# Second projection of both MLPs with the weights stationary and 400 tokens moving

## The reference, cut to what matters

```python
# layer 0
out = rmsnorm(attn_out, postnorm_w)
out = jax.nn.gelu(out @ mlp_w1 + mlp_b1) @ mlp_w2 + mlp_b2
return out + residual
# layer 2
h = _layer_norm(x, ln_mlp_scale, ln_mlp_offset)
h = jax.nn.gelu(h @ w_fc1 + b_fc1, approximate=False) @ w_fc2 + b_fc2
return x + h
```

## Time and profile before

| | |
|---|---|
| median of 3 runs | 4184.49 us (4182.9 to 4185.43) |
| the profiled execution | 4186.43 us, of which its span is 4184.7 us |
| mean granted clock of PE | 0.921 of full speed |
| PE, DVE, ACT, POOL busy | 85%, 39%, 28%, 13% of the span |
| first MLP: first matmul to end of last add | 616.2 to 780.5 us |
| second MLP: first matmul to end of last add | 3508.8 to 3672.4 us |

### The profile page before, as it was taken

The page is one execution under the profiler, slowest core; times in us unless marked ns, Lnnn a source line. Parts: engine busy times, 40 slices in busy tenths (PEclk is TensorE's granted clock), DMA queues, the critical chain, the costliest instruction groups (busy, mean ns, idle before and its releaser), DMA issues. The chain is left out here.

```text
span 4184.7 us, 50251 instructions
## 1 busy us (share of the span) xinstructions
PE 3566.8 (85%) x18055; PEld 2780.5 (66%) x18055; DVE 1639.4 (39%) x3090; ACT 1156.1 (28%) x2700; POOL 559.9 (13%) x479
## 2 busy tenths in 40 slices
PE   4999979796665789898998969989899997968886
PEld 3777758553333378787887858878787885846663
DVE  2454442316876232323223242232323324136654
ACT  2343343121002122222222222222222223235551
POOL 0000020023441300000000020000000001044432
PEclk9999989898987889999999979999999998977777
DMA  2111111000000041222222122121212212021101
GB/s 88 50 36 38 39 49 46 29 20 3 0 10 31 12 127 50 80 56 87 57 61 62 42 85 67 50 87 49 87 42 81 57 28 83 1 73 40 40 22 32
DMA packets 142028, 209.06 MB, mean 50 GB/s; under 512 B 18915, under 2 KB 104356, under 8 KB 141932
## 3 DMA queue, kind: packets, MB, share of 16 engines
q0 software_dynamic: 67584, 94.64, 8.7%
q1 hardware_dynamic: 74348, 113.17, 8.6%
HBM read 191.04 MB, written 13.47 MB: 49 GB/s over the span
## 5 line engine op out<-in xcount | busy, mean ns | idle before, releaser
L63 PE MATMUL work<-cT_layer_hi,wk_layer_hi 128*128 128x362 f32 x1024 | 390.3, 381 | 0.0
L1908 ACT ACTIVATE p_layer<-scores,neg_max_layer 100x362 f32<-100x362 f32 x256 | 144.3, 564 | 740.6 <-DVE neg_max_layer L1963 739.3
L64 PE MATMUL work<-cT_layer_lo,wk_layer_hi 128*128 128x362 f32 x1024 | 336.9, 329 | 0.0
L65 PE MATMUL work<-cT_layer_hi,wk_layer_lo 128*128 128x362 f32 x1024 | 336.6, 329 | 0.0
L1944 DVE TENSOR_TENSOR values_layer<-work,value_bias_layer 121x512 f32<-121x512 f32 x192 | 132.4, 690 | 519.4 <-PE work L65 519.4
L63 PE MATMUL work<-wv_layer_hi,cT_layer_hi 128*121 128x512 f32 x768 | 311.9, 406 | 0.0
L64 PE MATMUL work<-wv_layer_lo,cT_layer_hi 128*121 128x512 f32 x768 | 303.3, 395 | 0.0
L65 PE MATMUL work<-wv_layer_hi,cT_layer_lo 128*121 128x512 f32 x768 | 302.5, 394 | 0.0
L1751 POOL DMA_DIRECT2D cT_layer_hi<-ctxT_hi x64 | 47.7, 745 | 1745.6 <-PE work L65 1743.3
L1820 PE MATMUL o<-pT_layer,values_layer 121*128 121x100 f32 x1536 | 215.9, 277 | 56.9 <-ACT pT_layer L1914 56.9
L1820 PEld LDWEIGHTS o<-pT_layer,values_layer 121*128 121x128 f32 x1536 | 205.5, 191 | 87.5 <-ACT pT_layer L1914 70.2
(11 more groups left out here) (358 smaller groups left out, 7430.9 us busy)
## 6 DMA issues: line engine op xcount, KB each, us to landing
cT_layer_hi<-ctxT_hi POOLq DMA_DIRECT2D x64, 722.0 KB, 4.9
cT_layer_lo<-ctxT_lo POOLq DMA_DIRECT2D x64, 722.0 KB, 6.2
l0mlp_staged<-in_L_xattn_mlp_w_dram SPq DMA_DIRECT2D x16, 512.0 KB, 4.2
staged_layer<-in_L_xattn_wq_dram SPq DMA_DIRECT2D x8, 1024.0 KB, 5.2
staged_layer<-in_L_xattn_wk_dram SPq DMA_DIRECT2D x8, 1024.0 KB, 5.2
staged_layer<-in_L_xattn_wv_dram SPq DMA_DIRECT2D x8, 1024.0 KB, 5.2
staged_layer<-in_L_xattn_wo_dram SPq DMA_DIRECT2D x8, 1024.0 KB, 5.4
l2mlp_staged<-in_L_xattn_w_fc_dram SPq DMA_DIRECT2D x16, 512.0 KB, 4.2
```

Of the source, the lines that this page charges most:

```text
L63: pe.matmul(out, cut_a(a.hi), cut_b(b.hi), start=start, stop=False)
L64: pe.matmul(out, cut_a(a.hi), cut_b(b.lo), start=False, stop=False)
L65: return pe.matmul(out, cut_a(a.lo), cut_b(b.hi), start=False, stop=stop)
L1908: act.activation(probs[x % 4][:, 0:KEYS2], ps_scores[x % 2][0:L, 0:KEYS2], ACT.Exp, bias=neg_max[:, x:x + 1], accum_out=sums[:, x:x + 1]). ...
```

## The change

In `use` the two operands of the second projection change places: the weights `down_w` (128 hidden x 128 output features) are stationary, and the 400 tokens of a half move. For each of the 4 tiles of output features (`m`) and 2 tiles of hidden features there are 3 matmuls, so 24 as before. The sums then have output features on the partitions and must be turned back: at the end of a half ACT copies the banks m = 0, 2 and DVE the banks m = 1, 3 from PSUM to the first 400 columns of the four `staged` buffers (`copy_sums`); PE transposes them, 4 transposes for each batch, into a bank in the layout of `k.X` (`turn`); DVE adds that bank to `k.X` (`add`).

PSUM is dealt out anew: 3 banks for the first projection, 4 for the sums, 1 (`ps_token`) for the transposes. The first five batches use `ps_token` one after the other; the last three use the three banks of the first projection, which are then free. `turn` of the first half stands inside the steps 9 and 10, between the products: turn(0) and turn(1) in step 9 before use(8), turn(2) after it, turn(3) in step 10. Those of the second half stand at the end. `make` is called for one tile at a time, and waits for the gelu of tile n - 3. DVE's adds of the first half stand between its splits of `gT` in the steps 9 and 10 (`ADD_AT`).

```diff
--- before.py
+++ after.py
@@ -741,7 +741,9 @@
     CHUNK = 2
     CHUNKS = FT // CHUNK
     STEPS = HALVES * CHUNKS
-    STAGES = 4
+    STAGES = KT
+    UP = 3
+    ADD_AT = {(1, 0): [0], (1, 1): [1, 2], (2, 0): [3]}
 
     pieces = [("up", 0)]
     for c in range(CHUNKS):
@@ -753,8 +755,9 @@
         staged = [own.enter_context(nc.sbuf_tensor(f"{name}_staged{i}", [P, CHUNK * D], F32)) for i in range(STAGES)]
         g = [own.enter_context(nc.sbuf_tensor(f"{name}_g{i}", [P, HALF], F32)) for i in range(2)]
         gT = [Split(own, nc, f"{name}_gT{i}", [P, CHUNK, HALF]) for i in range(2)]
-        banks = psum_banks(nc, own, f"{name}_ps", 4)
-        sums = psum_banks(nc, own, f"{name}_sums", 4)
+        banks = psum_banks(nc, own, f"{name}_ps", UP)
+        sums = psum_banks(nc, own, f"{name}_sums", KT)
+        ps_token = psum_banks(nc, own, f"{name}_token", 1)
         loaded = [k.sems.take(f"{name}_loaded{i}") for i in range(STAGES)]
         w_rounded = k.sems.take(f"{name}_w_rounded")
         w_split = k.sems.take(f"{name}_w_split")
@@ -763,8 +766,15 @@
         g_rounded = k.sems.take(f"{name}_g_rounded")
         g_split = k.sems.take(f"{name}_g_split")
         used = k.sems.take(f"{name}_used")
+        copied_act = k.sems.take(f"{name}_copied_act")
+        copied_dve = k.sems.take(f"{name}_copied_dve")
+        token_turned = k.sems.take(f"{name}_token_turned")
         added = k.sems.take(f"{name}_added")
         block = own.enter_context(nc.Block())
+
+        def token_bank(b):
+
+            return ps_token[0] if b <= 4 else banks[b - 5]
 
         def piece_of(kind, c):
 
@@ -790,38 +800,64 @@
 
         @block.tensor
         def _(pe):
-            def make(step):
+            def make(step, f):
                 half, c = divmod(step, CHUNKS)
-                if half == 0:
+                if half == 0 and f == 0:
                     pe.wait_ge(w_split, pieces.index(("up", c)) + 1)
-                for f in range(CHUNK * c, CHUNK * (c + 1)):
-                    n = half * FT + f
-                    if n >= 4:
-                        pe.wait_ge(activated, n - 3)
-                    for t in range(KT):
-                        mm = product(pe, banks[n % 4][:, 0:HALF], up_w, hT, lambda x: x[:, t, f * P:(f + 1) * P],
-                                     lambda x: half_tokens(x, t, half), start=(t == 0), stop=(t == KT - 1))
-                    mm.then_inc(filled, 1)
+                n = step * CHUNK + f
+                if n >= UP:
+                    pe.wait_ge(activated, n - UP + 1)
+                col = (CHUNK * c + f) * P
+                for t in range(KT):
+                    mm = product(pe, banks[n % UP][:, 0:HALF], up_w, hT, lambda x: x[:, t, col:col + P],
+                                 lambda x: half_tokens(x, t, half), start=(t == 0), stop=(t == KT - 1))
+                mm.then_inc(filled, 1)
 
             def use(step):
                 half, c = divmod(step, CHUNKS)
                 if half == 0:
                     pe.wait_ge(w_split, pieces.index(("down", c)) + 1)
                 pe.wait_ge(g_split, CHUNK * (step + 1))
-                for b in range(4):
-                    if half > 0 and c == 0:
-                        pe.wait_ge(added, 4 * (half - 1) + b + 1)
+                if half > 0 and c == 0:
+                    pe.wait_ge(copied_act, KT // 2 * half)
+                    pe.wait_ge(copied_dve, KT // 2 * half)
+                for m in range(KT):
                     for f in range(CHUNK):
-                        mm = product(pe, sums[b][0:L, :], gT[step % 2], down_w, lambda x: x[:, f, b * L:(b + 1) * L],
-                                     lambda x: x[:, CHUNK * c + f, :],
+                        mm = product(pe, sums[m][:, 0:HALF], down_w, gT[step % 2],
+                                     lambda x: x[:, CHUNK * c + f, m * P:(m + 1) * P], lambda x: x[:, f, :],
                                      start=(c == 0 and f == 0), stop=(c == CHUNKS - 1 and f == CHUNK - 1))
                 mm.then_inc(used, 1)
 
+            def turn(b):
+
+                half, c = divmod(b, 4)
+                if c == 0:
+                    pe.wait_ge(copied_act, KT // 2 * (half + 1))
+                    pe.wait_ge(copied_dve, KT // 2 * (half + 1))
+                out = token_bank(b)
+                if b and out is ps_token[0]:
+                    pe.wait_ge(added, b if half == 0 else 4)
+                for m in range(KT):
+                    mm = pe.transpose(out[0:L, m * P:(m + 1) * P], staged[m][:, c * L:(c + 1) * L], k.ident[:])
+                mm.then_inc(token_turned, 1)
+
             for step in range(STEPS):
-                make(step)
+                make(step, 0)
+                if step == CHUNKS + 1:
+                    turn(0)
+                if step == CHUNKS + 2:
+                    turn(3)
+                make(step, 1)
+                if step == CHUNKS + 1:
+                    turn(1)
                 if step > 0:
                     use(step - 1)
+                if step == CHUNKS + 1:
+                    turn(2)
             use(STEPS - 1)
+            pe.wait_ge(activated, CHUNK * STEPS)
+            for b in range(4, B):
+                turn(b)
 
         @block.scalar
         def _(act):
@@ -830,6 +866,13 @@
                 weight, cut, view = piece_of(kind, c)
                 act.wait_ge(loaded[n % STAGES], 16 * (n // STAGES + 1))
                 weight.round(act, cut, view(staged[n % STAGES])).then_inc(w_rounded, 1)
+
+            def copy_sums(act, steps):
+                act.wait_ge(used, steps)
+                if steps > CHUNKS:
+                    act.wait_ge(token_turned, 4)
+                for m in range(0, KT, 2):
+                    act.activation(staged[m][:, 0:HALF], sums[m][:, 0:HALF], ACT.Copy).then_inc(copied_act, 1)
 
             round_piece("up", 0)
             for step in range(STEPS):
@@ -843,12 +886,15 @@
                     act.wait_ge(filled, n + 1)
                     if n >= 2:
                         act.wait_ge(g_split, n - 1)
-                    act.activation(g[n % 2][:], banks[n % 4][:, 0:HALF], func, bias=column(k, bias1, CHUNK * c + f)
+                    act.activation(g[n % 2][:], banks[n % UP][:, 0:HALF], func, bias=column(k, bias1, CHUNK * c + f)
                                    ).then_inc(activated, 1)
                     act.wait_ge(activated, n + 1)
                     if step >= 2:
                         act.wait_ge(used, step - 1)
                     gT[step % 2].round(act, lambda x: x[:, f, :], g[n % 2][:]).then_inc(g_rounded, 1)
+                if step > 0 and step % CHUNKS == 0:
+                    copy_sums(act, step)
+            copy_sums(act, STEPS)
 
         @block.vector
         def _(dve):
@@ -857,6 +903,18 @@
                 weight, cut, view = piece_of(kind, c)
                 dve.wait_ge(w_rounded, n + 1)
                 weight.rest(dve, cut, view(staged[n % STAGES])).then_inc(w_split, 1)
+
+            def copy_sums(steps):
+                dve.wait_ge(used, steps)
+                if steps > CHUNKS:
+                    dve.wait_ge(token_turned, 4)
+                for m in range(1, KT, 2):
+                    dve.tensor_copy(staged[m][:, 0:HALF], sums[m][:, 0:HALF]).then_inc(copied_dve, 1)
+
+            def add(b):
+                dve.wait_ge(token_turned, b + 1)
+                x = k.X[:, b, :]
+                dve.tensor_tensor(x, x, token_bank(b)[0:L, :], ALU.add).then_inc(added, 1)
 
             split_piece("up", 0)
             for step in range(STEPS):
@@ -869,11 +927,14 @@
                     n = step * CHUNK + f
                     dve.wait_ge(g_rounded, n + 1)
                     gT[step % 2].rest(dve, lambda x: x[:, f, :], g[n % 2][:]).then_inc(g_split, 1)
-                if c == CHUNKS - 1:
-                    dve.wait_ge(used, step + 1)
-                    for b in range(4):
-                        x = k.X[:, 4 * half + b, :]
-                        dve.tensor_tensor(x, x, sums[b][0:L, :], ALU.add).then_inc(added, 1)
+                    if half > 0:
+                        for b in ADD_AT.get((c, f), ()):
+                            add(b)
+                if step > 0 and c == 0:
+                    copy_sums(step)
+            copy_sums(STEPS)
+            for b in range(4, B):
+                add(b)
 
 
 def layer0_output(nc, k, ins, ctx, split):
```

## The result

| | before | changed |
|---|---|---|
| median | 4184.36 us (4182.9 to 4185.43, 4 runs) | 4156.64 us (4154.93 to 4158.6, 4 runs) |
| profiled execution, its span | 4186.43, 4184.7 us | 4157.48, 4155.7 us |
| mean granted clock of PE | 0.921 | 0.920 |
| first MLP, first matmul to last add | 164.34 us | 148.74 us |
| second MLP, the same | 163.63 us | 148.00 us |

A forecast was written before the change was run, and what follows sets the result against it. PE's matmul stream was taken to bound both MLPs. Per MLP -18.6 + 1.75 + 0.05 + 1.8 = -15.0 us, so -30.0 for two: from 4184.5 to 4154.5 us, range 4150 to 4162.

The forecast's parts named there:

- 1 products: Second projection's matmuls cost 0.1825 us each like those of make, with loads hidden: 18.6 us gained per MLP (18.1 to 18.8).
- 2 transposes in the middle: First half's 16 transposes per MLP, between products on busy PE, at 0.109 us each: 1.75 us added (1.4 to 3.5).
- 3 waits in the middle: Around each MLP's middle, only turn(1) is near its limit, with 0.2 us slack: 0.05 us added (0 to 1).
- 4 the end: After each MLP's last product, copies, transposes and adds take 4.30 us instead of 2.52: 1.8 us more (1.3 to 3.1).
- 5 stage behind, both MLPs: Stages after the MLPs start earlier and otherwise run as before: 0 us, -2 to +2 over both.
- Rival C: Weight loads do not hide under 400 columns in the second projection: 9.2 us per MLP come back, 4173 us; chance 0.02.
- D: Rival: granted clock falls inside the MLPs; 4271 us with all of the second projection at half clock; chance 0.01.
- E: Rival: gain is hidden behind ACT, DVE or the DMA, about 4180 us; chance 0.01.
- Rival B: In the middle, add(0) to add(2) each late, three waits up to 2.6 us: 7.8 per MLP, 4170 us; chance 0.03.
- Rival A: End transposes at half clock after a 1.2 us pause, stage behind colder too: 4.6 us less gain, 4159 us; chance 0.08.

The follow-up runs named there:

- before_400: Kernel before, old operand order, but only 400 of 512 output columns moving in the second projections (112 features left out); 4149.54 us, ratio 0.9913.
- no_turn: Changed kernel without copies and transposes, sums added in the wrong layout; 4146.90 us, ratio 0.9897 to the kernel before.
- turn_four: Changed kernel with every first-half transpose made four times, 48 more in each MLP; 4166.64 us, ratio 0.9953 to the kernel before.
- turn1_early: Changed kernel with turn(1) directly behind turn(0), ahead of the 12 products between them; 4161.45 us, ratio 0.9940 to the kernel before.
- wq_early: Changed kernel with layer 3's Wq fetched in the second half of the second MLP; 4148.42 us, ratio 0.9912 to the kernel before.
- before_wq: Kernel before with layer 3's Wq fetched in the second half of the second MLP; 4188.47 us, ratio 1.0005.
- wq_again: wq_early run once more without edit, in the same rounds as before_wq; 4147.65 us, ratio 0.9914 to the kernel before.
- first_only: Changed kernel with the old function kept in the second MLP, so only the first has the change; 4169.85 us, ratio 0.9964 to the kernel before.
- tail_split: Changed kernel with the last use done by feature tiles, copies and transposes going out during the next tile's products; 4154.32 us, ratio 0.9922 to the kernel before.
- both: Changed kernel with the edits of tail_split and wq_early together; 4155.46 us, ratio 0.9926 to the kernel before.

## Why the prediction was right

By its own steps, for one MLP:

| step | predicted | measured |
|---|---|---|
| 1 products | -18.6 | -19.5 (16 x (9.92 - 8.70)) |
| 2 transposes in the middle | +1.75 | +1.76 (4 x 0.44) |
| 3 waits in the middle | +0.05 | +0.05 |
| 4 the end | +1.8 | +1.97 |
| sum | -15.0 | -15.7; the stretches say -15.6 and -15.6 |
| 5 stage behind, both MLPs | 0 (-2 to +2) | +2.2 |

**The products** were priced from the form that they would take, and have its price: 0.181 where 0.1825 was read. The 0.9 us more is that small distance, over `use` (0.5) and `make` (0.5) alike. It puts the term outside its stated bounds, 18.1 to 18.8, which counted only the spread of `make` in the old stream. In the kernel before a `make` between products of 512 columns took 4.38 us; among its own kind it takes 4.35, and so does `use`. Rival C (loads not hidden) is excluded by before_400 and no_turn, D (half clock in the MLPs) by PEclk 1.00, E by PE's 127.00 of 127.

**The transposes in the middle** came out as read from the earlier trace rows, and turn_four shows that price on a larger number. They were 0.35 each group and 0.09 on the product behind it, so the term was right as the sum of two things that I had not told apart.

**The waits**: turn(1) had no slack of 0.2 us but none. PE's arrival was right: T is 694.51, and it reached turn(1) at T + 4.81 (said: 4.82). But the add that frees the bank ended at T + 4.76, not T + 4.6, and 0.05 of PE's time was lost. The chain had been timed from the wrong row: the matmul at 645.44 is the first of the next tile (L63), and the tile's last one, for which gelu waits (L65), stands ahead of it:

```profile
645.25 0.34 PE L65 MATMUL l0mlp_ps<-l_hT_hi,l0mlp_up_lo 128*128 128x400 f32 x1
```

From its start gelu comes after 0.39 us and the split after 1.58, where the prediction had 0.20 and 1.39. The changed kernel has the same distance, from this row to the split at 698.09:

```profile
696.51 0.35 PE L65 MATMUL l0mlp_ps<-l_hT_hi,l0mlp_up_lo 128*128 128x400 f32 x1
```

Read rightly, the chain ends at about T + 4.8, and the forecast slack is nothing. That the cost stayed at the 0.05 of the table is luck: 0.2 us more in the chain would have been waited for. turn1_early shows what the 12 products between turn(0) and turn(1) are there for: without them 2.0 us per MLP. Rival B needed all three waits late; turn(2) and turn(3) had their slack.

**The end** is 0.17 longer than priced. Copies begin 0.04 behind the last product and the pair on DVE takes 1.05, as said; but 0.26 pass from its end to the first transpose (I had 0.05), and the transposes (0.61) and adds (2.49) are as said. The handover behind DVE's copy was mis-sized.

**The stage behind** is where the small error lies. Behind the first MLP the 0 holds as far as it can be seen: the last of the 32 transposes that open layer 1 starts 14.6 us behind the last add in both kernels. Behind the second the prediction had "otherwise as before", and weighed only that the clock may fall elsewhere. At full clock the transposes of `X` were 1.66 us quicker, but nothing came of it, since Wq, issued at the start of the stage and just hidden behind them before, came last. Then its fetch took 6.2 us instead of 5.1, which makes the first product 1.1 us later; in turn_four, with the same stage and a fetch of 5.3 us, it comes 7.05 us behind the last add, nearly the 6.9 of the kernel before. Why the fetch is longer in three of these four profiles (6.2, 6.4, 6.3; 5.3 in turn_four) no run shows. The other 1.2 us are the products, which run at half clock for longer behind the pause of 4.7 us. wq_early and before_wq show that both parts go with Wq: taking it away is worth 5.6 us in the one stage and nothing in the other. The step's 0 was 2.2 us too good and its bound of 2 just short (0.9 to 2.3 over the four profiles); with the products' 0.9 per MLP on the other side, most of it cancelled, so the total is nearer than its parts: 29.0 us by the two profiles and 27.7 by the medians, for 30.0. (One slip of the sums: the chances of all that is clearly faster add up to 0.98 and not 0.97.)

Rival A, a colder end, did not come for the transposes: in 762 to 763 PEclk is 1.00, and behind the second MLP through 3644. Its other half, a colder stage behind, did come behind the second MLP, though by the wait for Wq and not by the pause ahead of the transposes. By the Trainium skill, "TensorE: Matmul & The Clock Gate", Part 4, "PE-mode transpose", transposes don't count as PE being busy. In six profiles of six with 16 transposes behind the last product (the changed kernel twice, turn_four, turn1_early, wq_early, wq_again) `X`'s transposes all ran at full clock, in 2.7 us; in the five without them (the kernel before, first_only in its second MLP, before_400, no_turn, before_wq) they took 4.2 to 5.2. In wq_early and wq_again 9.8 us lie between the last product of the MLP and the first of the next stage, with nothing on PE but 48 transposes and three pauses, and the clock is 1.00 all the time; in the kernel before it fell at 3673.6, 3.7 us behind the last product. The runs speak against the rule. That the 16 transposes held the clock is the likely reading, but no run adds them and changes nothing else.

Left open: why the clock fell in tail_split and both, where PE has less idle time ahead of the transposes of `X` (0.16 and 1.43 us) than in the changed kernel (1.35 and 1.53), but does half of its turning between products; why Wq's fetch varies; and where the 6 us of scatter between the MLPs come from. No run tells these apart.
